# A graph network kernel: node degrees as one more column of a dense layer, and a first product that takes its resident blocks first

## The reference

```python
x = _layernorm(x + _L0_gnn_ref(...))      # edge MLP, summed by dst
x = _layernorm(x + _L1_gnn_ref(...))      # GIN layer, below
x = _layernorm(x + _L2_gnn_ref(...))      # 3 products with the weighted adjacency
x = _layernorm(x + _L3_gnn_ref(...))      # 10 products with the same matrix

# _L1: aggr = segment_sum(relu(x[src] + edge_attr @ We + be), dst)
h = (1.0 + eps_gin) * x + aggr
h = jax.nn.relu(h @ W1 + b1) @ W2 + b2
h = jnp.where(h >= 0, h, 0.2 * h)
h = (h - mean(h)) / sqrt(var(h) + 1e-5) * gamma + beta

# _L2: deg = segment_sum(edge_weight, col), dinv = rsqrt(deg) where deg > 0, else 0
#      x <- dinv[col] * sum of edge_weight * dinv[row] * x[row], three times
# _L3: deg_out by rows, deg_in by columns, both with a loop of weight 1; ten steps
#      h <- 0.9 * agg + 0.1 * feat
```

## Time and profile before

| | |
|---|---|
| median of 3 runs | 2695.18 us (2695.15 to 2700.47) |
| the profiled execution | 2692.2 us |
| its span, first to last instruction | 2690.4 us |
| TensorE busy | 2607.0 us, 97% |
| VectorE busy | 1788.8 us, 66% |
| GpSimd busy | 1169.4 us, 43% |
| ScalarE busy | 420.2 us, 16% |
| streamed matrix pieces | 312 loads of 1024 KB, 8.8 us to landing in the median |

### The profile page before, as it was taken

How to read it: one execution, slowest core, us unless ns; L and a number is a source line. 1 busy time by engine, 2 the same in 40 slices (tenths; PEclk the granted TensorE clock), 3 DMA queues, 4 the chain that set the end, 5 groups by cost and what they waited for, 6 DMA issues and landing times.

```text
span 2690.4 us, 59886 instructions
## 1 busy us (share of the span) xinstructions
PE 2607.0 (97%) x18663; PEld 1739.0 (65%) x18663; DVE 1788.8 (66%) x3713; ACT 420.2 (16%) x1080; POOL 1169.4 (43%) x1235
## 2 busy tenths in 40 slices
PE   6899999999999799999999999899999999999998
PEld 5688888888888578888888888533333333333333
DVE  4688888888888599999999999796531111111114
ACT  2122222222222211111111111200100000000001
POOL 4466666666666367777777777200000000000000
PEclk9899999999999799999999999799999999999999
DMA  4222222222222333333333333299999999999997
GB/s 110 52 62 60 60 60 60 61 60 60 59 61 60 61 69 86 77 77 77 78 78 79 78 93 80 83 348 365 341 336 346 351 350 350 351 346 353 359 345 268
DMA packets 376595, 447.32 MB, mean 166 GB/s; under 512 B 154575, under 2 KB 193589, under 8 KB 373290
## 3 DMA queue, kind: packets, MB, share of 16 engines
q1 hardware_dynamic: 323834, 376.76, 43.0%
q0 software_dynamic: 38784, 39.79, 8.0%
q10 hardware_dynamic: 13920, 30.00, 3.0%
HBM read 416.03 MB, written 30.36 MB: 166 GB/s over the span
## 4 chain that ended last, share of the span: by engine, by line
PE 94%; DVE 2%; DMA 1%; ACT 1%; SPq 1%; issue 0%; DVEq 0%; ACTq 0%
PE bank L1577 31%; PE bank L1778 31%; PE bank L1600 11%; PE bank L1589 7%; PE bank L1564 4%; PE bank L1568 3%; PE bank L1749 2%; PE bank L1553 2%; PE bank L1782 1%; DMA arena<-in_edge_weight 1%; SPq L572 0%; PE bank L1736 0%; PE bank L1720 0%; ACT arena L1493 0%; PE bank L1714 0%
## 5 line engine op out<-in xcount | busy, mean ns | idle before, releaser
L1778 PE MATMUL bank<-arena 128*64 128x512 f32 (+1 forms) x4368 | 889.0, 543 | 12.7 <-DVE arena L1087 10.6
L1577 PE MATMUL bank<-arena 128*128 128x320 bf16 x6090 | 882.2, 301 | 8.7 <-DVE arena L840 8.7
L1577 PEld LDWEIGHTS bank<-arena 128*128 128x128 bf16 x6090 | 599.1, 98 | 250.1 <-DVE arena L840 8.9
L658 POOL DMA_INDIRECT arena<-d_p,arena x606 | 573.7, 947 | 299.4 <-issue 240.2
L658 POOL DMA_INDIRECT arena<-d_t,arena x606 | 572.8, 945 | 212.5 <-issue 207.2
L1778 PEld LDWEIGHTS bank<-arena 128*64 128x64 f32 x4368 | 316.2, 136 | 496.7 <-issue 464.3
L1185 DVE TENSOR_TENSOR arena<-bank,arena 128x256 f32<-128x256 f32 (+1 forms) x70 | 27.8, 396 | 572.6 <-PE bank L1749 572.5
L1600 PE MATMUL bank<-arena 128*128 128x150 f32 x2352 | 333.0, 290 | 0.0
L1600 PEld LDWEIGHTS bank<-arena 128*128 128x128 f32 x2352 | 317.8, 189 | 5.3
L847 DVE SCALAR_TENSOR_TENSOR bank<-arena,bank 128x320 f32<-128x320 f32 x404 | 222.7, 552 | 142.5 <-PE bank L1577 142.5
L840 DVE TENSOR_TENSOR arena<-arena,bank 128x1280 bf16<-128x1280 f32 x203 | 299.4, 1475 | 0.0
(11 more groups left out here) (209 smaller groups left out, 1592.9 us busy)
## 6 DMA issues: line engine op xcount, KB each, us to landing
arena<-d_w SPq DMA_DIRECT2D x312, 1024.0 KB, 8.8
arena<-d_code SPq DMA_DIRECT2D x203, 128.0 KB, 3.0
d_w<-arena ACTq DMA_DIRECT2D x24, 1024.0 KB
arena<-in_edge_attr SPq DMA_DIRECT2D x101, 128.0 KB
arena<-d_p,arena POOLq DMA_INDIRECT x606
arena<-d_t,arena POOLq DMA_INDIRECT x606
arena<-d_rec SPq DMA_DIRECT2D x588, 4.0 KB
arena<-d_q SPq DMA_DIRECT2D x202, 11.8 KB
```

The source lines that it names most:

```text
L658: g.indirect_dma_start(G[:, b, j, 0:F], None, table, bass.IndirectOffsetOnAxis(ap=idx[:, b, j:j + 1], axis=0)).then_inc(r.g[b], 16)
L1577: last = t.matmul(psY[g], SOH[:, g, a_, :], X[:, a_, z, :, :], start=a_ == z == 0, stop=a_ == SLICES - 1 and z == PARTS - 1)
L1778: last = t.matmul(banks[t_ % 4][F * (n % 2):F * (n % 2) + F, 0:w_], old[:, n, :], right, start=n < 2, stop=False)
```

## The change

- `h1T` gets rows 64 to 95 of ones (a VectorE memset of 32x3200, in the place of GpSimd's of 1x3200) and row 96 (`DEGROW`), a copy of the degree row of `aggT` made by GpSimd. `w2n` gets 97 rows: its row 96 is zero but for a one in column 64; rows 65 to 95 are zero. So column 64 of a block's second-layer output is the degree. The 25 degree matmuls, `sel` and the copy on VectorE go. ScalarE copies the degrees out of banks 3 to 7 after the last leaky step.
- The norm buffers move out of the ring's range: `endA` is `xs[1]`, `endB` is `comb`, `endS` lies where `gb` begins. The first six loads are issued at other points.
- VectorE's steps get another order: part 0 first, up to its xs, and most of part 1 behind it.
- The first product takes the nine resident blocks of its first four chunks ahead of all streamed ones. Their transposes (of the chunk before) then stand directly behind that chunk.

```diff
-NC_DEG, NC_XSA, NC_X2, NC_XS = 33, 47, 51, 52
+NC_LEAKY, NC_DEG, NC_XSA, NC_X2, NC_XS = 22, 30, 37, 50, 51
+DEGROW = 96
...
-        w2n = at(o_l1 + F, HALF, parts=F + 1)
+        w2n = at(o_l1 + F, HALF, parts=DEGROW + 1)
...
+        endA, endB = xs[1], comb
+        endS = at(top[0], 8, NB)
...
-            sp.wait_ge(s.nc_t, NCT_DEG)
-            for j in range(3):
+            sp.wait_ge(s.nc_t, 1)
+            for j in range(2, RING - 1):
                 load_piece(j)
-            sp.wait_ge(s.nc_v, NC_X2)
-            for j in range(3, RING):
+            sp.wait_ge(s.l1z, 6)
+            sp.wait_ge(s.nc_t, H1_AT[6])
+            for j in range(2):
                 load_piece(j)
+            sp.wait_ge(s.nc_t, H2_AT[4])
+            load_piece(RING - 1)
...
-            g.memset(sel[F:F + 1, 0:1], 1.0).then_inc(s.l1z, 1)
+            g.memset(w2n[DEGROW:DEGROW + 1, F:F + 1], 1.0).then_inc(s.l1z, 1)
...
-            g.memset(h1T[F:F + 1, :], 1.0).then_inc(s.l1z, 1)
+            g.tensor_copy(h1T[DEGROW:DEGROW + 1, :], aggT[F:F + 1, :]).then_inc(s.l1z, 1)
             pool.wait_ge(s.ld_l1, 7 * 16)
-            pool.wait_ge(s.l1z, 5)
+            pool.wait_ge(s.l1z, 6)
...
+            d.memset(h1T[F:DEGROW, :], 1.0).then_inc(s.l1z, 1)
...
+            act.wait_ge(s.nc_v, NC_LEAKY)
+            for g5 in range(5):
+                a.activation(nsc[:, 0, 5 * g5:5 * g5 + 5].unsqueeze(2), banks[3 + g5][:, 0:5 * HALF].rearrange("p (a c) -> p a c", c=HALF)[:, :, F:F + 1],
+                             ACT.Copy).then_inc(s.nc_a, 1)
...
-                    last = t.matmul(banks[3 + g5][:, HALF * n:HALF * n + HALF], h1T[0:F + 1, lo_:lo_ + P], w2n, start=True, stop=True)
+                    last = t.matmul(banks[3 + g5][:, HALF * n:HALF * n + HALF], h1T[0:DEGROW + 1, lo_:lo_ + P], w2n, start=True, stop=True)
...
-            pe.wait_ge(s.l1z, 5)
+            pe.wait_ge(s.l1z, 6)
             second_layer(0)
...
-            pe.wait_ge(s.nc_a, RELU_AT[6])
-            for n in range(NB):
-                last = t.matmul(banks[0][:, n:n + 1], aggT[:, P * n:P * n + P], sel[:, 0:1], start=True, stop=True)
-            last.then_inc(s.nc_t, 1)
...
+                if first:
+                    pe.wait_ge(s.nc_v, NC_XSA)
+                    for t_, c in enumerate(CORDER[:4]):
+                        w_ = CH if c < NCH else LASTW
+                        for n in range(RES):
+                            t.matmul(banks[t_][F * (n % 2):F * (n % 2) + F, 0:w_], old[:, n, :], Wres[:, n, CH * c:CH * c + w_],
+                                     start=n < 2, stop=False)
+                    pe.wait_ge(s.nc_v, NC_XS)
                 for t_, c in enumerate(CORDER):
...
-                    for n in range(NB):
-                        if first and t_ == 0 and n in (0, LNP[1][0]):
-                            pe.wait_ge(s.nc_v, NC_XS if n else NC_XSA)
+                    if first and 0 < t_ < 4:
+                        turn_chunk(k, t_ - 1)
+                    for n in range(RES if first and t_ < 4 else 0, NB):
```

More of the change, by code:

```diff
@@ L1088, in first_xs @@
                                       nsc[:, 7, lo_:lo_ + n].unsqueeze(2).to_broadcast([P, n, F]), ALU.mult))
-            for g5 in range(2):
-                leaky(g5)
+            leaky(0)
+            leaky(1)
             centre(0)
             assert cnt[0] == SQ1[0]
+            leaky(2)
             variance(0, SQ1_A[0])
             assert cnt[0] == SD1[0]
-            scaled(0, SD1_A[0], lnB)
+            scaled(0, SD1_A[0], endB)
             residual(0)
             assert cnt[0] == SQ2[0]
-            for g5 in range(2, 5):
-                leaky(g5)
+            leaky(3)
+            leaky(4)
+            assert cnt[0] == NC_LEAKY
+            variance(0, SQ2_A[0])
+            assert cnt[0] == SD2[0]
             centre(1)
             assert cnt[0] == SQ1[1]
-            variance(0, SQ2_A[0])
-            assert cnt[0] == SD2[0]
-            variance(1, SQ1_A[1])
-            assert cnt[0] == SD1[1]
-            v.wait_ge(s.nc_t, NCT_DEG)
-            link2(d.tensor_copy(nsc[:, 0, :], banks[0][:, 0:NB]))
+            v.wait_ge(s.nc_a, NCA_DEGC)
             link2(d.tensor_scalar(nsc[:, 2, :], nsc[:, 0, :], 1.0, None, ALU.add))
@@ L1123, in _ @@
             assert cnt[0] == NC_XSA
+            variance(1, SQ1_A[1])
+            assert cnt[0] == SD1[1]
+            scaled(1, SD1_A[1], endB)
+            residual(1)
+            assert cnt[0] == SQ2[1]
             variance(1, SQ2_A[1])
```

40 lines of the change are left out of this document (18 added, 22 removed).

## The result

Beside each other on one chip the changed kernel took 2719.57 us (median of 4 runs, 2719.17 to 2719.89), the kernel before 2695.16 (4 runs, 2692.57 to 2700.47): ratio 1.0089, 95% interval 1.0077 to 1.0102. Forecast were 2689.6 and a range up to 2694.0. The result lies 25.6 us above the range.

The account below looks back on a forecast made before the run. The time was taken to go by when the first product starts and how long TensorE's gapless product takes. Gain 9.8 - 1.6 - 2.6 = 5.6 us; 2692.2 becomes 2686.6, or 2689.6 against the 2695.18 median; range 2685.5 to 2694.

Parts of the forecast that it names:

- the sum: Whole kernel: 9.8 us earlier start less 1.6 for turns and 2.6 for pieces, 5.6 us gained, unchanged from the second product on.
- the removal: Second layer: dropping the 25 degree matmuls, 10.53 us on TensorE, gains little; VectorE stands only 1.4 us for them.
- the one on the slower side: Rival (c), GpSimd's degree-row copy: it takes up to 10.2 us or the memset holds it off; 2696.1 to 2699 us, chance 0.07.
- The copied row: GpSimd ahead of the second layer: the degree-row copy takes 3.7 us and delays the start by 0.9; VectorE's memset costs nothing.
- VectorE's new order: VectorE ahead of the first product: first xs part done at 1729.5 against 1739.27, 9.8 us earlier.
- Rival (b): Ahead of the first product: copy takes 6.0 us, or TensorE's clock falls early, costing up to 3; 2692 us, chance 0.20.
- All of xs at the old time: VectorE's second normalisation: all of xs done at 1743.2 against 1743.6, almost the same.
- Three turns: TensorE in the first product: three chunk turns lose their cover, gaps of 0.73, 0.33 and 0.73 us, 1.6 us net cost.
- The streamed pieces: First product: late pieces stall TensorE 2.6 us, bounds 0 and 4, because VectorE must first sum earlier pieces.
- TensorE never waits for the second part: First product: resident blocks take 15.3 us, over the 13.7 that VectorE needs for the second xs part, so no wait.
- Block 20 of the second product: Second product: TensorE reaches it at X+87.8, VectorE's last xs comes at X+84.1; no wait, 3.7 us of room.
- rival (d): First and second product: VectorE's chain is the real bound, TensorE only waits; gain 0.4 us, 2694.8 us, chance 0.06.

Follow-up runs that it names:

- c1: The placed kernel with VectorE's row sums of the first product's 24 streamed pieces replaced by writes of 1.0; ratio 0.9978 to the kernel before.
- d1: The placed kernel plus unread transposes on TensorE, eight ahead of the first layer and more in the wait for xs; 2688.10 us, ratio 0.9975 to the kernel before.
- d4: The placed kernel plus only the eight unread transposes ahead of the first layer; 2689.39 us (one run), where the kernel before takes 2694.52.
- e1: The placed kernel timed a third time, in another series; 3183.28 us against 3186.70 for the kernel before, ratio 0.9990.
- e2: The placed kernel plus only the eight unread transposes ahead of the first layer, in e1's series; 3180.93 us, ratio 0.9990 to the kernel before.
- b2: The placed kernel with the first product in the kernel before's order of blocks; 3184.22 us, ratio 1.0003 to the kernel before.
- placed kernel: The changed kernel with TensorE's loop code back where the kernel before had it, by never-executed waits; ratios 0.9985, 0.9989 and 0.9990 to the kernel before.
- fillers in both: d1 against the kernel before with the same kind of unread transposes ahead of the first layer and in the wait for xs; 2688.10 against 2691.26 us.
- a1: The changed kernel with 398 instead of 200 never-executed waits, putting TensorE's loop code where the kernel before had it; 3144.60 against 3148.61 us, ratio 0.9985.
- b1: The placed kernel timed a second time, in another series; 3179.92 us against 3184.78 for the kernel before, ratio 0.9989.

## Why the prediction was wrong

The step that failed is this sentence of the sum: "From the second product on nothing has changed, and TensorE has no gap, so it stays." Nothing that is executed changed there, and the gaps that TensorE does have from there on (4.6 us in all before) are the same in both kernels. But I had taken 100 instructions off TensorE's program ahead of a loop, and had costed the removal at nothing because those matmuls ran beside VectorE's work. Their place in the program had a worth that no timeline shows: it held the loop where its body touches seven blocks and not eight. Lost: 27.7 us, three jumps of 9.0 to 9.7. None of the rivals held it; the one on the slower side looked for it in GpSimd. It could have been seen: instruction loads were in the trace of before, and that they stop during the loop's later rounds says that it fits, but not by how much.

The Trainium skill (Runtime: NRT & Kernel Launch, "Instruction fetch mechanics") says that instructions come in blocks of 16 KiB fetched in sequence, that TensorE's memory for them holds 128 KiB, and that a taken branch to code outside the present window makes the engine fetch before it goes on. The traces agree with the loads of 16384 bytes and with the stop behind the jump. It also speaks of a window of two pages; here a body that touches seven blocks stays resident, so for that the measurement decides. Eight blocks are those 128 KiB; why a body that touches eight is lost already, no run shows.

The other steps:

- **The copied row.** Forecast 3.7 us for the copy and a delay of 0.9. The copy took 2.85. In the changed kernel's profile TensorE does not wait, since the half clock made its first layer longer; in the five profiles of the new order with a late fall (c1, d1, d4, e1, e2) it waits 0.44 or 0.45 us, and for VectorE's memset, which the sum had at nothing: it starts 0.72 us behind VectorE's step before it and ends after the copy. The second layer starts 3.24 us after the first layer's start there, 2.83 before: a delay of 0.4, so 0.5 better than forecast. The figure by the Trainium skill (GPSIMD Engine Reference, section 3.1), 2.75, was nearer than mine. The Trainium skill's rule that the memset does not contend with GpSimd (SBUF — State Buffer, "Who interferes with whom") agrees with the traces: 2.85 us beside the memset, near the 2.76 of the old memset alone.
- **VectorE's new order.** Forecast 9.8 us earlier; 9.7 with the fall at +6.1 in both kernels, 10.1 with late falls at unlike moments. Right. In the two profiles shown only 3.9 are left, since the clock fell 7.4 us sooner against the stage's start in the second. Rival (b) named that fall and its price of up to 3 us, but as a result of the copy. It is chance, and it was already in the profile that I worked from: a late fall, in an execution 3.0 us under the median.
- **All of xs at the old time.** Right but for the clock: 1749.0 in place of 1743.2. In e1, with its late fall, they are done 40.3 us after the first layer's start; the forecast is 40.7 on that count.
- **Three turns.** 0.77, 0.31 and 0.69 us of idle time, forecast 0.73, 0.33, 0.73.
- **The streamed pieces.** Forecast 2.6 us in one or two gaps; in the mean 2.8 by the chunks (1.1 to 5.0) and 2.0 by the named waits, in one to three gaps. c1 shows VectorE's sums to be the cause.
- **TensorE never waits for the second part.** Right where the clock is at 0.50 in the resident phase. In d1, where it is at 1.00, the first streamed block starts 13.7 us after X, not 12.4, as xs ends: it waits some 1.3 us. With the old first product (b2) it stands 7.6 us.
- **Block 20 of the second product.** No wait: the first chunk of product 1 takes 11.50 or 11.51 us in every profile, so rival (d) is out.
- **The sum.** Forecast 5.6 us; 6.2 and 5.2 by the profiles, 3.8 by the times of the placed kernel, 3.2 with fillers in both. The mechanism holds for the stage; the times give some two thirds of the size.

The result is those few microseconds, less 27.7.

## What to carry to other kernels

Where an edit adds or removes instructions ahead of a long hardware loop, count the blocks of the instruction loads that the loop's body touches from where it starts, and look whether the trace of before stops loading inside the loop: if it does, the loop may fit by luck, and an edit far away can undo it. Look first at idle time that ends in "issue" and at the queue of instruction loads when a kernel gets slower everywhere but where it was edited; waits in a branch that is never entered show in one run whether placement is the cause. And compare two profiles of a stage only after their clocks are compared, for one execution is one draw of the moment at which it falls.

## What the runs showed that I had not expected

- A loop of 1588 TensorE instructions ran four rounds with no load after its first at three placements (seven blocks touched), and was loaded anew each round at two others (eight), at 4.2 to 9.7 us a jump; written out, its code came in at no cost that the run shows.
- The granted clock fell within 1.1 us of the first layer's start in 13 of the 20 profiles and 6.1 to 16.4 us after it in the other seven, with identical programs on both sides (a1 and b1 early, e1 late), and X followed it by 7 us.
- With transposes in the wait for xs the clock was back at 1.00 ahead of the first product in all three kernels that had them, after a fall at +1.0, +6.1 and +14.8; without them it was at 0.50 there in all 17 other profiles.
